# Second attention: all four last scatters of a sentence's rows behind the next-but-one sentence's first unit

## The reference, cut to what matters

```
x = x + attn_a(layernorm(x))     # 16 heads of 64, causal, ALiBi
x = x + ffn(layernorm(x))        # 8 experts, each row takes its best 2
x = x + attn_b(layernorm(x))     # 8 heads of 128, causal, rotary embedding
x = x + ffn(layernorm(x))        # the same 8 experts
```

```
q, k, v = x @ w_aq, x @ w_ak, x @ w_av        # per head; rope on q and k
p = softmax(q @ k.T / 128, masked above the diagonal)
r = sum over heads of (p @ v) @ w_ao
```

## Time and profile before

| | us |
|---|---|
| median of 3 runs | 2169.72 |
| lowest and highest of them | 2169.67, 2174.20 |
| the profiled execution's own time | 2171.33 |
| its span, first to last instruction | 2169.4 |
| second attention with its lead-in and end, as the trace shows it | about 1225 to 1930 |
| granted TensorE clock over the span | 0.975 of full speed |

### The profile page before, as it was taken

One profiled execution on the slowest core, in us unless ns is written; L12 is line 12 of the kernel. 1 busy time (PEld: TensorE's weight loads), 2 busy tenths in 40 slices (PEclk: granted clock), 3 DMA queues, 4 the chain that ended last, 5 costly groups with the idle time before them and its releaser, 6 DMA issues.

```text
span 2169.4 us, 39456 instructions
## 1 busy us (share of the span) xinstructions
PE 2033.1 (94%) x11622; PEld 1630.8 (75%) x11622; DVE 1551.0 (71%) x4607; ACT 1436.3 (66%) x3761; POOL 1138.2 (52%) x1342
## 2 busy tenths in 40 slices
PE   7899999999999999899999999898998989889995
PEld 5677777777777777688877788686777777668884
DVE  7877777777777777578777776666675756647877
ACT  5777777777777786645546776676676757555445
POOL 4665555555555555535335746565655655434432
PEclk9999999999999999999999999999999999999998
DMA  4344412021202010534442432222221212243548
GB/s 135 137 143 145 144 32 93 32 92 32 92 32 93 32 52 11 207 93 136 124 150 76 147 100 87 66 77 83 76 91 53 87 37 71 96 146 111 155 130 278
DMA packets 76647, 215.55 MB, mean 99 GB/s; under 512 B 12692, under 2 KB 47796, under 8 KB 73496
## 3 DMA queue, kind: packets, MB, share of 16 engines
q1 hardware_dynamic: 63480, 176.58, 25.1%
q0 software_dynamic: 12960, 36.46, 4.8%
HBM read 155.51 MB, written 128.81 MB: 131 GB/s over the span
## 4 chain that ended last, share of the span: by engine, by line
PE 74%; DVE 12%; ACT 7%; issue 3%; POOL 2%; DMA 2%; SPq 0%; ACTq 0%; DVEq 0%; POOLq 0%
PE bank L630 6%; PE bank L650 5%; PE bank L2291 5%; PE bank L612 5%; PE bank L1539 4%; PE bank L597 3%; PE bank L2265 3%; PE bank L2267 3%; PE bank L2266 3%; PE bank L598 3%; PE bank L1524 3%; PE bank L1440 2%; PE bank L1441 2%; PE bank L1442 2%; PE bank L543 2%
## 5 line engine op out<-in xcount | busy, mean ns | idle before, releaser
L1158 POOL TENSOR_TENSOR P<-P,rc 128x128 f32<-128x128 f32 (+3 forms) x512 | 359.1, 731 | 345.8 <-DVE rc L956 345.7
L948 DVE CUSTOM_DVE_ANT_0 P<-bank,tab 128x512 f32<-128x512 f32 (+3 forms) x512 | 241.1, 485 | 107.3 <-PE bank L598 103.6
L773 ACT ACTIVATE P<-P,mn 128x128 f32<-128x128 f32 (+3 forms) x512 | 281.7, 552 | 33.0 <-DVE mn L948 29.2
L2582 POOL DMA_INDIRECT yD<-Yf,place x142 | 140.4, 989 | 257.0 <-ACT Yf L2367 244.7
L784 ACT COPY PT<-bank 128x512 f32<-128x512 f32 (+1 forms) x384 | 194.0, 516 | 101.4 <-PE bank L612 94.2
L2043 POOL TENSOR_TENSOR q<-rf,q 128x512 fp32r<-128x512 f32 x128 | 162.9, 1295 | 168.9 <-ACT q L1658 168.7
L2032 POOL TENSOR_TENSOR rf<-rp 128x512 f32<-128x512 f32 x128 | 165.8, 1296 | 145.8 <-DVE rp L1862 145.0
L612 PE MATMUL bank<-cst,P 128*128 128x128 f32 x1280 | 207.3, 277 | 15.6 <-POOL P L1158 9.9
L597 PE MATMUL bank<-q 128*128 128x512 f32 (+3 forms) x512 | 184.8, 372 | 15.9 <-DVE mn L948 11.5
L612 PEld LDWEIGHTS bank<-cst,P 128*128 128x128 f32 x1280 | 152.5, 141 | 43.4 <-POOL P L1158 14.4
L924 DVE TENSOR_TENSOR q<-bank,q 64x512 fp32r<-64x512 f32 x256 | 175.7, 687 | 7.2 <-ACT q L764 1.3
(11 more groups left out here) (266 smaller groups left out, 5906.4 us busy)
## 6 DMA issues: line engine op xcount, KB each, us to landing
hS<-in_c_fill SPq DMA_DIRECT2D x128, 544.0 KB, 4.0
Gf<-hS SPq DMA_DIRECT2D x142, 136.0 KB
yg<-yD SPq DMA_DIRECT2D x14, 512.0 KB, 5.0
X<-in_x SPq DMA_DIRECT2D x8, 512.0 KB, 5.2
stage<-in_w SPq DMA_DIRECT2D x8, 512.0 KB, 3.7
w1hD<-W1A SPq DMA_DIRECT2D x8, 512.0 KB
w1lD<-stage SPq DMA_DIRECT2D x8, 512.0 KB
rD<-xn SPq DMA_DIRECT2D x8, 512.0 KB, 3.0
```

Of the source, the lines that this page charges most:

```text
L773: i = e.activation(ps, ps, ACT.Exp, bias=mn[:, pb, t:t + 1], scale=-1.0, accum_out=rs[:, pb, t:t + 1])
L948: e.tensor_tensor_reduce(out=P[:, pb, OFF[t]:OFF[t] + w], in0=score(h, t), in1=tab[:, 512 - w:512], scale=-SLOPES[h % 16], scalar=3e38, op ...
L1158: i = e.tensor_tensor(ps, ps, rc[:, h % 3, t:t + 1].broadcast_to([128, w]), ALU.mult)
```

## The change

On POOL's list in the second attention, sentences 2 to 7: the scatters n = 4 and 5 stay where they were, at the end of unit 0; n = 6 and 7 come to stand right behind them in unit 0, where they had stood at the end of unit 1.

```diff
@@ -2074,8 +2074,8 @@
                         if bt and p > 5:
                             for n in (2 * p - 12, 2 * p - 11):
                                 put_rows(e, q, 1, bt - 1, n, hh)
-                        elif bt > 1 and p < 2:
-                            for n in (2 * p + 4, 2 * p + 5):
+                        elif bt > 1 and p == 0:
+                            for n in range(4, 8):
                                 put_rows(e, q, 1, bt - 2, n, hh)
```

## The result

The changed kernel takes 2119.61 us (median of 4 runs, 2113.43 to 2120.52), the kernel before in the same comparison 2170.48 (4 runs, 2169.67 to 2174.20). The ratio is 0.9756, 95% interval 0.9734 to 0.9778: 51 us less. The profiled execution took 2113.43 us, its span is 2111.5. It is the fastest of the four, so its trace shows some 6 us more gain than the median does.

The account below looks back on a forecast made before the run. ACT, held in order by a late-issued scatter, was taken to stall PE. 41.8 + 10.6 = 52.4 us, less 1.7 for the clock, gives 50.7 off 2171.33: 2120.6, and 2119.0 by the median 1.6 lower; range 2112 to 2131.

Parts of the forecast that it names:

- What bounds it: Second attention: ACT waits 52.8 us in six pieces for a late-issued scatter before writing `hh`; PE stands 39.4 us.
- (1): POOL, unit 0: the four scatters fit into its idle time, ending 2.06 us before POOL is wanted; added cost 0.
- (2): Before ACT writes `hh`: the moved scatters have landed 5 to 8 us before ACT comes.
- (3): At `gate_in`: `xl` and r2 are ready before ACT comes, the later by 1.37 us, so no second wait stands.
- my margin of 3.4 us: POOL, unit 0: may be delayed by 2.06 + 1.37 = 3.4 us before `gate_in` waits.
- The worth on PE: L1539 of unit 1 to unit 2, against sentence 1: 41.8 us for sentences 2 to 6, 10.6 for 7, sum 52.4.
- What the clock takes back: Later units, sentences 2 to 6: two clock falls of 1.7 us, one more than before, so -1.7 us.
- the known place: Around 1304 to 1312 in sentence 1, where the clock is 0.79; sentences 1 and 5 of 1 to 6 show it.
- A: PE clock, second attention: ten more falls of 1.7 us take back 17 us, time 2134, with half 2126; chance 0.11.
- B: POOL, unit 0: third scatter held until the first has landed, costing 7 us over six sentences, time 2126; chance 0.06.
- C: POOL, unit 0: scatters held one by one until the previous lands, losing some 50 us, time 2219; chance 0.02.
- D: ACT's wait stays as long because another of its conditions is met only then; time 2166 to 2174; chance 0.02.

Follow-up runs that it names:

- six operations: Changed kernel with six small POOL operations on an unread tile behind the four scatters of unit 0, second attention, sentences 2 to 7: 2144.73 us, ratio 0.9883.
- `gate_in` moved: Kernel before, scatters unmoved, ACT's `gate_in` moved from the end of unit 1 to behind the exponentials of unit 2: 2148.52 us, ratio 0.9900.
- the deviation first: Changed kernel with six extra small POOL operations in unit 0, and unit 1's deviation moved ahead of `low` on POOL's list: 2139.20 us, ratio 0.9856.

## Why the prediction was right

The forecast was 2119.0, the measurement 2119.6. Step by step:

*What bounds it.* Borne out from three sides: later scatters cost 19 us, an earlier last one gains 5, and taking ACT's copies out from behind the wait gains 20 with POOL's list untouched.

*(1) The four fit into unit 0.* Predicted 2.06 us of idle time behind them, measured 2.07.

*(2) They have landed when ACT comes.* No wait for a landing at L1712 in any of the six sentences. Sentence 7's four landed within 3.2 us of their issue, ahead of the load, as said.

*(3) Nothing else is late.* True for this change, but my margin of 3.4 us for POOL was on the wrong path. I had taken r2, which `gate_in` needs itself. What gives way first stands behind the deviation and L1845 on DVE's list: the rotary products and the maximum for which PE's scores wait (1.79 us with six operations), and beside it the reciprocal and ACT's scale (0.61 us). The 0.3 us that I called slack in the expectations was ACT's wait for the reciprocal, and no slack. With POOL 0.9 us late nothing was lost, with 3.9 us 27. The slack behind POOL's idle time is about 1.0 us and not 1.37. At my margin of 3.4 us I would have forecast no cost; by these rows it would have cost an estimated 0.4 us a sentence, and what the clock adds.

*The worth on PE.* 41.8 for sentences 2 to 6, measured 41.9; 10.6 for sentence 7, measured 10.7. Taking another sentence without the stall as the model was exact to 0.03 us each. The charge of 1.0 for the listing was 0.93 in unit 1; units 2 and 3 of sentence 7 are 1.0 longer than before on top, which I had not charged.

*What the clock takes back.* Predicted -1.7 us. In both profiled executions of the changed kernel the known place is free of it in all sentences, +3 against the profile of before, so the term's sign was wrong in these two. In the run with the first attention changed as well, the same second attention has it in four sentences, where before had two; there the sign is right. The price of 1.7 for one fall was 1.3 to 1.6. How many sentences are hit differs from execution to execution, as the prediction said, and that the sum hit the median to 0.6 us is in part luck, since single executions lie 8 us apart.

*The rivals.* A: not in the two profiles of the changed kernel; its first half, the known place in sentences 2 to 6, is there in four of the five in the run just named, and with `gate_in` moved. Its second half, one more fall in each of the six, was not seen. B and C: four scatters in a row keep their pitch of 1.27 us and 0.96 us each. (The 0.53 us in their sums stand in no row; without them B and C come out a little milder.) The rule of the Trainium skill cited for B ("SBUF — State Buffer", "A bandwidth-pool intuition that's wrong"), 3.1 us for a DMA issue that VectorE holds up, is not shown by the trace: the scatters of the changed second attention took 0.96 to 1.22 us. D: the wait is gone.

## What to carry to other kernels

When an engine waits in order for a transfer, ask where the transfer's issue stands on its own engine's list. It can be late though its engine is idle, and the last of a group sets the whole wait. Price the repair by a twin in the same trace that has the work without the wait; idle time alone leaves out what the clock loses behind it. And before calling an engine's slack free, follow every result that it produces there, not only the one that the waiting instruction names, and on each engine that takes one, what stands behind it on that engine's list. The same move was worth 51 us in one stage and nothing in the other.

## What the runs showed of the hardware

A DVE operation beside a POOL operation can be much longer. L1845's `TENSOR_SCALAR` of 128x256 takes 0.41 us as a rule. In the run with the deviation first, the two of four that ran beside POOL's `low` took 1.38 and 1.36 us in sentence 4, the two behind it 0.40 each, 3.31 in all. The Trainium skill ("SBUF — State Buffer", "Who interferes with whom") says that the two engines share a pair of ports, and that beside a VectorE instruction in a two-port mode, which `tensor_scalar` can take, whichever is first holds the pair for its whole instruction. The trace agrees in kind: each of the long ones began some 0.1 us after a POOL operation of 1.3 us had begun, and ended 0.16 us behind its end. Which mode they took no run shows.

The clock of TensorE fell from 2.4 to 1.2 GHz behind the idle pieces of 6.2 us in sentences 2 to 6, mean 0.79 to 0.80 over the stretch. In unit 1 of the run with six operations, with idle pieces of 0.6 and 1.8 us, it fell in sentences 3 and 5 and not in 2, 4 and 6. Behind two pieces of 0.9 and 0.5 us in unit 4 it fell in some executions and not in others, at the same place of the same work.
